# Both halves of the attention product side by side in the first two query units

## What is computed

```python
q = feature_map(split(x @ Wq.T + bq), orf)      # exp of a projection minus a norm
k = feature_map(split(x @ Wk.T + bk), orf)
v = split(x @ Wv.T + bv)
kv = jnp.einsum('nlm,nld->nmd', k, v)
ksum = jnp.sum(k, axis=1)
buf = jnp.concatenate([kv, ksum[..., None]], axis=-1)
out = jnp.einsum('nlm,nmd->nld', q, buf)
out = out[..., :-1] / out[..., -1:]             # the denominators
x = _layernorm(x + out.reshape(...) @ Wo.T + bo)
x = _layernorm(x + x @ (w_ternary * scale).T)
```

## Time and profile before

| | |
|---|---|
| median of 3 runs | 1286.36 us (1285.94 to 1286.54) |
| the profiled execution | 1285.8 us |
| its span in the trace | 1284.0 us |
| busy: PE, DVE, ACT, POOL | 98%, 70%, 56%, 28% |
| granted TensorE clock | 0.999 of full speed |

### The profile page before, as it was taken

The page is one execution under the profiler, slowest core; times in us unless marked ns, Lnnn a source line. Parts: engine busy times, 40 slices in busy tenths (PEclk is TensorE's granted clock), DMA queues, the critical chain, the costliest instruction groups (busy, mean ns, idle before and its releaser), DMA issues.

```text
span 1284.0 us, 24908 instructions
## 1 busy us (share of the span) xinstructions
PE 1258.4 (98%) x8626; PEld 957.5 (75%) x8626; DVE 898.3 (70%) x1615; ACT 713.5 (56%) x1435; POOL 363.5 (28%) x745
## 2 busy tenths in 40 slices
PE   9999999999999999999999999999999999999986
PEld 8767787777877678776787768876788767886665
DVE  6588765786668775787657786577765777656766
ACT  5657536574356743667337663367544665356634
POOL 0113332124311333213422134311352123421143
PEclk9999999999999999999999999999999999999999
DMA  7658314772146821566215762267602675036611
GB/s 239 152 132 224 91 45 118 185 188 75 58 124 166 201 60 53 139 177 174 62 58 135 196 152 70 62 146 199 164 31 71 161 202 143 34 92 150 160 39 66
DMA packets 82748, 160.32 MB, mean 125 GB/s; under 512 B 17856, under 2 KB 36416, under 8 KB 82112
## 3 DMA queue, kind: packets, MB, share of 16 engines
q1 hardware_dynamic: 68880, 139.78, 43.5%
q10 hardware_dynamic: 9648, 16.85, 3.5%
q0 software_dynamic: 4096, 2.11, 0.7%
HBM read 39.13 MB, written 16.78 MB: 44 GB/s over the span
## 4 chain that ended last, share of the span: by engine, by line
PE 86%; ACT 5%; issue 2%; DVE 2%; POOL 0%; ACTq 0%; POOLq 0%; DVEq 0%
PE ps L952 25%; PE ps L915 21%; PE ps L965 9%; PE ps L1015 8%; PE ps L983 5%; PE ps L970 4%; PE ps L938 4%; PE ps L940 4%; PE ps L939 4%; PE ps L1041 2%; ACT features L675 2%; ACT squares L658 1%; ACT x_hi L643 1%; PE ps L992 1%; DVE stats L773 0%
## 5 line engine op out<-in xcount | busy, mean ns | idle before, releaser
L675 ACT ACTIVATE features<-ps 128x512 f32<-128x512 f32 x512 | 278.4, 603 | 176.6 <-PE ps L965 128.4
L825 DVE SCALAR_TENSOR_TENSOR unit_lo<-ps,cols,unit_hi 128x512 fp32r<-128x512 f32 x128 | 95.2, 743 | 116.7 <-ACT squares L658 116.7
L965 PEld LDWEIGHTS ps<-orf_stack,stacks 98*128 98x128 f32 x1024 | 130.8, 191 | 27.9 <-issue 20.3
L915 PE MATMUL ps<-Wo_hi,stacks 128*128 128x512 f32 x448 | 150.4, 402 | 0.0
L648 ACT ACTIVATE values_then_attention<-ps 128x512 f32<-128x512 f32 x64 | 38.3, 599 | 194.8 <-PE ps L940 191.6
L567 POOL CAST norm_rows<-norms_turned 128x32 fp32r<-128x32 f32 x64 | 16.5, 257 | 443.4 <-DVE norms_turned L843 443.4
L789 DVE TENSOR_TENSOR den<-den,features 128x512 f32<-128x512 f32 x186 | 127.9, 688 | 10.8 <-ACT features L675 0.5
L965 PE MATMUL ps<-orf_stack,stacks 98*128 98x128 f32 x1024 | 130.4, 272 | 0.0
L551 POOL TENSOR_SCALAR stats<-stats 128x1 f32<-128x1 f32 x128 | 36.3, 283 | 330.5 <-DVE stats L776 330.3
L1015 PE MATMUL ps<-features,kv_ksum 128*32 128x512 f32 x1024 | 123.1, 598 | 4.7 <-ACT features L675 2.2
L656 ACT ACTIVATE unit_hi<-ps,cols 128x512 fp32r<-128x512 f32 x128 | 88.4, 690 | 65.6 <-PE ps L952 65.6
(11 more groups left out here) (132 smaller groups left out, 2596.7 us busy)
## 6 DMA issues: line engine op xcount, KB each, us to landing
stacks<-unit_hi SPq DMA_DIRECT2D x512, 128.0 KB, 2.4
stacks<-unit_lo SPq DMA_DIRECT2D x256, 128.0 KB, 2.7
out<-rows ACTq DMA_DIRECT2D x56, 256.0 KB, 2.0
rows<-in_x_t SPq DMA_DIRECT2D x49, 256.0 KB, 3.1
rows<-in_x SPq DMA_DIRECT2D x32, 256.0 KB, 4.2
features<-in_x SPq DMA_DIRECT2D x32, 256.0 KB, 3.9
values_then_attention<-in_x_t SPq DMA_DIRECT2D x8, 256.0 KB, 6.7
stacks<-norm_rows POOLq DMA_DIRECT2D x128, 16.0 KB, 2.7
```

The costliest lines, as they stand in the source:

```text
L675: nc.scalar.activation(FE[:, n % 8, :, 0:M], ps[:, :].rearrange("p (a m) -> p a m", a=HG), ACT.Exp, scale=C_EXP).then_inc(a_exp.sem, 1)
L825: nc.vector.scalar_tensor_tensor(out=EL[:, u % 2, half], in0=ps[:, :], scalar=BC[:, u:u + 1], in1=EH[:, u % 2, half].bitcast(F32), op0=ALU ...
L915: last = mm(out, a, b, start=(n == 0), stop=(n == len(terms) - 1))
L965: last = mm(ps[:, M * h:M * (h + 1)], slot[0:QK, L * h + P * r:L * h + P * (r + 1)], ORF[0:QK, h, :], start=True, stop=True)
```

## The change

In the list of the units u = 1 and u = 3, in all eight batches, `p[3]` moves ahead of the first half of the product, the second half moves right behind the first, and `q1` comes after both. For that the second half's denominators go to a bank of the feature ring (2, 3 or 4) in place of bank 7, and this holds in every query unit, the unmoved ones too. PE's second half no longer waits for the first half's denominators to be read. The next user of the ring bank waits for DVE's turn of the second half's denominators instead. The number of instructions stays the same on every engine.

```diff
         elif u < NU - 3:
-            seq += kv + f(2, 3) + p[1] + [("KVT", b, g)] + q0 + f(4, 5) + p[2] + s1 + l1 + f(6, 7) + [("GG", b, g, 0)]
-            seq += p[3] + q1 + [("GG", b, g, 1)] + norm + lift + [("R", b, g, 0)]
+            seq += kv + f(2, 3) + p[1] + [("KVT", b, g)] + q0 + f(4, 5) + p[2] + s1 + l1 + f(6, 7)
+            seq += p[3] + [("GG", b, g, 0), ("GG", b, g, 1)] + q1 + norm + lift + [("R", b, g, 0)]
...
+    if stage[0] == "GG":
+        return (2, 3, 4) if stage[3] else None
     return RING.get(stage[0])
...
+            if kind == "GG":
+                return v_dt, v_dt.nth(b, 2 * k + 2)
...
-                    nc.vector.transpose(turned[:, :, 0:DH], DN[:, :].rearrange("p (a c) -> p a c", c=DH)).then_inc(v_dt.sem, 1)
+                    dens = ps if h else DN
+                    nc.vector.transpose(turned[:, :, 0:DH], dens[:, :].rearrange("p (a c) -> p a c", c=DH)).then_inc(v_dt.sem, 1)
...
                     if half == 0:
 
                         pe.wait_ge(a_kv.sem, a_kv.nth(b, g + 1))
+                        pe.wait_ge(v_dt.sem, v_dt.nth(b, 2 * g))
                     else:
...
-                    pe.wait_ge(v_dt.sem, v_dt.nth(b, 2 * g + half))
                     pe.wait_ge(a_exp.sem, a_exp.nth(b, 16 * g + 8 + 4 * half + 4))
-                    for bank, c in ((DN, P), (ND[half], 0)):
+                    for bank, c in ((ps if half else DN, P), (ND[half], 0)):
```

## The result

| | before | after |
|---|---|---|
| median | 1286.36 us (1285.94 to 1287.94, 5 runs) | 1292.46 us (1290.73 to 1292.49, 5 runs) |
| ratio | | 1.0041, 95% interval 1.0027 to 1.0055 |
| profiled execution | 1285.8 us, span 1284.0 | 1290.73 us, span 1288.9 |

The changed kernel is slower by 0.4%, some 6 us in the medians and 4.9 us between the two profiled executions. The forecast was 1291.0 us (1287.5 to 1293.5), and 1290.4 for the profiled execution.

A forecast was written before the change was run, and what follows sets the result against it. PE, busy 1258.4 of 1284.0 us, was taken as the bound. Places gave 0.8 + 1.8 + 2.3 - 0.3 = +4.6 us on 1285.8: 1290.4 profiled, median 0.56 higher, 1291.0 us; range 1287.5 to 1293.5, 8 times in 10.

The forecast's parts named there:

- What bounds the kernel: Whole kernel: PE is busy 1258.4 of 1284.0 us, so time is won on PE's starts and lost when PE waits.
- PE's gain, 0.31 us per unit: Feature-matmul pair to next unit's first `F`, u=1 and u=3: 5.56 us instead of 5.87, 16 units, 4.9 us in all.
- half 0 to half 1: Start of one product half to start of the next on PE: taken as 1.77 us, at most 1.86; no row showed it.
- DVE's loss, 1.15 us: DVE behind both halves: `Q` of half 1 no longer runs in a gap, so `R` starts 1.15 us late.
- Margin against lateness: At L992, last add against PE's need: lateness 1.15 us against margin 1.12; PE follows by 0.06, so +0.09 at nine places.
- The four places with a smaller margin: At L992, four places with margin 0.75 us: +0.46 each, +1.8 us in sum.
- hitch: One DVE chain instruction starting some 0.35 us late at four places; assumed to stay at its place in DVE's queue.
- The last batch's u=5: One place with a projection ahead of `G`, margin 2.5 us at L992: PE keeps its gain, -0.3 us.
- The other three kinds of place: Nine places +0.09 each (+0.8 us), four +0.46 each (+1.8), two in the first batch +1.15 each (+2.3).
- What the ring bank costs and the lost wait for bank 7 brings: Last batch, u=5 and u=6: 0.89 us wait removed, ring-bank wait added; costed at nothing, since `G` follows `R`.
- The gain reaches the end: Rival: PE keeps 0.31 us 16 times, and 0.9 in the last batch; 1280.5 us, or 1281.4 without that; chance 0.07.
- Lost and won cancel: Rival: tighter add chain or more overlap of halves; with lateness 0.9 us, total +0.9, 1287.3 us; chance 0.15.
- The lateness spreads further up: Rival: PE's waits for `L` and at L992 add up, another 0.3 us per place; +9 us, 1296 us; chance 0.08.

The follow-up runs named there:

- experiment 2: Changed kernel with q1 (DVE's squares) moved ahead of p[3] and both product halves; 1282.22 us, ratio 0.9953.
- experiments 1: Changed kernel with q1 put back between the two halves on DVE, PE's order kept; 1283.74 us against 1287.24 for before, ratio 0.9968.
- experiment 6: Kernel before with one more DVE instruction, its result unread, behind the turn of the norms in u=1 and u=3; 1289.2 us against 1286.54, ratio 1.0015.
- experiment 3: Kernel before with only q1 moved behind the second half of the product, PE's order and banks kept; 1296.47 us, ratio 1.007.
- Experiment 4: Changed kernel with the old list of stages, so against before only the bank of the second half's denominators differs; 1287.01 us, ratio 0.9995.
- second trace of the changed kernel: Changed kernel run again unaltered, for another trace and more runs beside before; 1292.78 us against 1286.54, ratio 1.0051.
- experiment 5: Changed kernel with q1, norm and lift all moved ahead of p[3] and both halves; 1282.82 us, ratio 0.997.
- experiment 7: Kernel before with q1 ahead of p[3] and both halves adjacent, both halves' denominators still in bank 7; 1299.19 us, ratio 1.0105.

## Why the prediction was right, point by point

**What bounds the kernel.** Held: PE loses as soon as it waits, and the place where it waits is L992/L997.

**PE's gain, 0.31 us per unit.** 0.33 in the unit, 0.27 as it arrives at L997. The term that no row showed, half 0 to half 1, was taken as 1.77 (four rounds of 0.44 are 1.76); from the block it is 385.28 - 381.71 - 1.86 = 1.71, if half 1 to `F` is still 1.86, and DVE's two turns of the denominators start 1.72 us apart (383.70 and 385.42). That the whole came out as forecast, 5.54 against 5.56, is in part luck: the six projection matmuls took 1.18 (380.21 to 381.39) in place of 1.15, which makes up for half of it. The rule on the change of tiling mode (the Trainium skill, TensorEngine Tiling (Array Packing), section Tiling Modes) agrees in kind with the unit here; that the gain would reach the end as well was wrong for the changed kernel and right for experiment 2. No run here sets such a change apart from the rest of the order, so what one costs isn't shown.

**DVE's loss, 1.15 us.** The stretch from the second half's denominators to `R` was to be 1.15 + 0.68 + 0.72 + 0.14 = 2.69; it is 2.70. In the first batch, where nothing covers it, 1.14 and 1.13 us arrive.

**Margin against lateness.** This was the step that decided. The changed kernel (1.15) and experiments 1, 6 and 3 (0.40, 0.59, 1.46) bear it out with four sizes of lateness: each of the 15 places at L992 or L997 loses what exceeds its margin, and in the changed kernel PE followed the last add by 0.05 or 0.06 us at all 15. The place in the last batch, where PE waits for `L`, comes out some 0.1 us later than this rule gives. With its margin of 0.65 us (`L` ended at 1198.94 in the kernel before and the projection started at 1199.59) and 0.06 us from `L` to PE, the rule gives -0.19, 0.00 and +0.87 in experiments 1, 6 and 3; measured are -0.09, +0.13 and +0.97. The PE row below shows the matmul behind the wait 0.50 us long where its like is 0.40; why it is longer, no run shows.

**The four places with a smaller margin.** Three lost 0.40 to 0.45, against 0.46. The fourth lost 0.08: its hitch stood in the kernel before at the turn of the norms, and the order behind it is another now. The guess that a hitch stays with its place in DVE's queue held three times of four. In experiment 6, where DVE has one instruction more per unit, all four were gone. What makes the hitches is open; no run here was made to find it.

**The last batch's u=5: wrong.** The forecast had PE keep its 0.31 us, as the adds are 2.5 us early. It overlooked another wait on the same DVE chain. The projection ahead of `G` there needs the bank that `L` frees, and `L` stands two adds from the end of the chain. DVE, then PE, last batch of the kernel after:

```profile
1203.37 0.74 DVE L829 SCALAR_TENSOR_TENSOR unit_lo<-ps,cols,unit_hi 128x512 fp32r<-128x512 f32 x1
```

```profile
1204.17 0.50 PE L957 MATMUL ps<-x_hi,Wq_hi 128*128 128x512 f32 x1 [0.70 <-DVE unit_lo L829]
```

`L` ends at 1204.11 and PE goes on at 1204.17: +0.63 instead of -0.31. The error is 0.9 us. The other three kinds of place came out 0.6 us lower than forecast together (0.2 at the nine, 0.4 at the four), so that 4.6 forecast meets 4.9 measured by luck as well as by the mechanism.

**What the ring bank costs and the lost wait for bank 7 brings: nothing.** Experiment 4 shows that the two come to nothing together. The reason given was half right: the wait for the ring bank, 0.74 us, does show in u=6 of the last batch, but `G` stands behind that wait and the two `F` after it, and not behind `R`, which ends 0.14 us earlier. In the kernel before `R` was not the last either: from half 1 at 1211.25 to `G` at 1216.04 the timeline shows PE without idle time, and `R` ended at 1215.89.

**The rivals.** The gain reaches the end: it does once the squares are moved (experiment 2), with 1282.2 us where the rival had 1280.5 to 1281.4, but not in the changed kernel. Lost and won cancel: it wanted the lateness to be 0.9; it was 1.15. The lateness spreads further up: PE waits for `L` at three places of the changed kernel, 0.38 and 0.37 us in the first batch and 0.70 in the last, and at none in the kernel before. But the waits don't add up, as the argument against this rival said: in the first batch the two waits together let 1.14 and 1.13 us arrive, the lateness once, and in the last batch the wait for `L` takes the place of that at L997. The line of the first of them, in u=2 of the first batch:

```profile
78.14 0.50 PE L957 MATMUL ps<-x_hi,Wq_hi 128*128 128x512 f32 x1 [0.38 <-DVE unit_lo L829]
```

**The time.** The sum was made against the profiled execution and hits it: 1290.4 to 1290.73. The median is 1.7 us above that execution, which the 0.56 us of before did not foresee. So of the 6.1 us between the medians the mechanism is shown for 4.9; for the rest, see the clock below.

## What to carry to other kernels

When work is regrouped on the busiest engine, ask what the same list does to the engines that are not: an instruction that ran for nothing in a gap can land in a chain without one, and then it costs its full length less the margin at the end of the chain. So measure two things ahead: how late the chain starts, and how early its last result is at each place that waits for it, at every place and for every result, not only the last one. And if the regrouping is sound, the cheap repair is to move the displaced instructions into the gap that the new order opens, here ahead of `p[3]` and the product, for some 10 us between the medians of the changed kernel and of experiment 2.

## What the runs showed of the hardware that was not expected

**TensorE's clock fell inside the product in some executions.** In the second trace of the changed kernel PE stood idle for 1.61 us ahead of the product in u=5 of the last batch, as in every trace (1.61 or 1.62), and then ran the first half at the lower of its two levels. PE's timeline, then busy times and granted clock in stretches (stretch, length, busy us and instructions of PE, PEld, DVE, ACT, POOL, clock, DMA share, GB/s) of that trace and of the first one:

```profile
1214.01 5.19 PE L1020 MATMUL ps<-features,kv_ksum 128*32 128x512 f32 x32 [1.61 <-ACT kv_ksum L700]
```

```profile
1214.00:1217.30 3.30, 3.29 (x17) 0.79 (x21) 0.28 (x1) 0.93 (x2) 0.00 (x0) 0.52 0.87 199
```

```profile
1213.00:1216.40 3.40, 3.26 (x32) 0.94 (x32) 1.60 (x5) 1.06 (x3) 0.00 (x0) 1.00 0.86 193
```

At a granted clock of 0.52, nearly all of the stretch at 1.2 and not 2.4 GHz, the block of 32 records took 5.19 us in place of 3.64. The profiled execution of experiment 5 shows the same at the same place (5.34 us), that of before and of experiments 1, 2 and 4 do not. It would account for most of the 1.7 us by which the median of the changed kernel is above its profiled execution. Where the clock fell in an execution without a trace isn't known, but its mean granted clock is on record. The traces with a mean of 0.999 (the kernel before, experiments 1 to 4 and 7) show it below full speed only in their last 5 us. The three with 0.998 have one more fall each: two at the product, and the first trace of the changed kernel near its end (0.90 from 1270 to 1275 us and 0.76 to 1280), where it costs little, since from the last L997 to the end it is 81.35 us against 81.15 before. None of the changed kernel's ten executions has a mean above 0.998; of the 36 of the kernel before that ran beside the experiments, 22 have 0.999 (median 1286.5 us) and 14 have less (1288.4 us). So with the changed kernel falls were more frequent, and a part of the difference between the medians can come from them. Why the order of the stages should bear on it, no run shows.

**The start of the program varies.** The 48 records of warm-up matmuls took 7.43 us in the trace of before, 6.95 in that of after, 7.18 in experiment 2 and 8.47 in experiment 5, and all of PE's work starts by as much earlier or later. Why it varies is not shown. A difference of about 1 us between two profiled spans should not be read as an effect of an edit. The steps from place to place can be, as they repeated within 0.06 us in two traces of the changed kernel.
